# Low parts of the later experts' weights formed on GpSimd instead of VectorE, the opening tile's down weights split in two pieces, and the last tiles' table numbers read early on TensorE

## The reference, cut to what matters

```python
scores = sigmoid(xf @ gate_w + bias)
top_scores, top_idx = top_k(scores, 2)
w = zeros((T, 8)).at[arange(T)[:, None], top_idx].add(top_scores / (sum(top_scores) + 1e-06))
hact = gelu(einsum('th,ehi->tei', xf, up_w) + up_b)          # h = 256, i = 1024
eo = einsum('tei,eih->teh', hact, down_w) + down_b
combined = einsum('teh,te->th', eo * 0.1, w)
shared = (gelu(xf @ sw_up + sb_up) @ sw_down + sb_down) * 0.1
out = shared + combined
out = out / (max(abs(out), axis=-1) + 1e-06)
x = x + gb * out
```

## Time and profile before

| | us |
|---|---|
| median of 3 runs | 867.51 |
| lowest and highest of them | 866.81 and 871.16 |
| the profiled execution, device time | 869.19 |
| its span in the trace | 867.40 |

### The profile page before, as it was taken

The page is one execution under the profiler, slowest core; times in us unless marked ns, Lnnn a source line. Parts: engine busy times, 40 slices in busy tenths (PEclk is TensorE's granted clock), DMA queues, the critical chain, the costliest instruction groups (busy, mean ns, idle before and its releaser), DMA issues.

```text
span 867.4 us, 21209 instructions
## 1 busy us (share of the span) xinstructions
PE 830.5 (96%) x5973; PEld 777.6 (90%) x5974; DVE 612.7 (71%) x1570; ACT 454.6 (52%) x857; POOL 455.6 (53%) x519
## 2 busy tenths in 40 slices
PE   5999999999999999999989999989999999999993
PEld 5778887889899889888889999989999999999993
DVE  5688988567877687677776667657666667665664
ACT  3765565144444444443666556656555566655550
POOL 4354420124656655765503655554666665665675
PEclk9899999899999999999999999999999999999997
DMA  8220000090422432240671332352344443344543
GB/s 303 75 88 11 0 1 1 12 320 16 125 51 76 125 91 59 100 125 20 227 272 51 102 101 78 90 176 68 86 91 98 94 89 87 77 97 92 101 100 54
DMA packets 68392, 83.08 MB, mean 96 GB/s; under 512 B 22916, under 2 KB 56670, under 8 KB 68192
## 3 DMA queue, kind: packets, MB, share of 16 engines
q0 software_dynamic: 25696, 39.77, 19.7%
q1 hardware_dynamic: 41808, 41.64, 15.3%
q10 hardware_dynamic: 816, 0.79, 0.3%
HBM read 45.43 MB, written 41.29 MB: 100 GB/s over the span
## 4 chain that ended last, share of the span: by engine, by line
PE 59%; issue 6%; DMA 4%; DVE 4%; POOL 3%; ACT 2%; DVEq 1%; ACTq 1%; POOLq 0%; SPq 0%
PE psY L2000 15%; PE psUp L1975 15%; PE psU L1188 10%; PE psY L1200 9%; DMA gx<-shared_part,meta 2%; PE psZ L1128 1%; PE psO L1128 1%; DMA shared_part<-ys,widx 1%; PE psH L1941 1%; ACT gu L2044 1%; PE psZ L1116 1%; POOL out L2320 1%; PE psZ L1107 1%; PE psU L1151 1%; PE psZ L1138 1%
## 5 line engine op out<-in xcount | busy, mean ns | idle before, releaser
L1975 PE MATMUL psUp<-eT,wup 128*128 128x256 f32 x1632 | 204.4, 285 | 7.2 <-DVE eT L2101 4.7
L1975 PEld LDWEIGHTS psUp<-eT,wup 128*128 128x128 f32 x1632 | 200.3, 193 | 8.4 <-issue 8.1
L2000 PE MATMUL psY<-wdn,gTh 128*128 128x256 f32 x1088 | 200.5, 286 | 0.0
L2000 PEld LDWEIGHTS psY<-wdn,gTh 128*128 128x128 f32 x1088 | 169.4, 192 | 0.0
L2000 PE MATMUL psY<-wdn,gTl 128*128 128x256 f32 x544 | 154.3, 284 | 0.0
L2320 POOL DMA_INDIRECT out<-fin,oidx x68 | 109.2, 1606 | 25.4 <-issue 17.5
L2296 POOL DMA_INDIRECT gx<-shared_part,meta x68 | 67.3, 989 | 92.8 <-DMA shared_part<-ys,widx 63.7
L2044 ACT ACTIVATE gu<-psUp,ubias 128x256 f32<-128x256 f32 x272 | 113.4, 468 | 4.4 <-DVE gTl L2106 3.4
L2063 ACT ACTIVATE ys<-yc,meta 128x256 f32<-128x256 f32 x66 | 30.0, 503 | 152.1 <-DVE yc L2129 152.1
L2306 POOL DMA_INDIRECT shared_part<-ys,widx x66 | 68.9, 1044 | 71.8 <-issue 44.6
L2106 DVE TENSOR_TENSOR gTl<-gu,gTh 128x512 fp32r<-128x512 f32 x136 | 93.7, 689 | 18.2 <-ACT gTh L2049 15.6
(11 more groups left out here) (331 smaller groups left out, 1399.4 us busy)
## 6 DMA issues: line engine op xcount, KB each, us to landing
hin<-expert_in SPq DMA_DIRECT2D x36, 256.0 KB
X<-in_L_attn_x SPq DMA_DIRECT2D x8, 512.0 KB, 7.6
X<-bo_row POOLq DMA_DIRECT2D x8, 512.0 KB, 5.6
shared_part<-prow SPq DMA_DIRECT2D x8, 512.0 KB, 5.9
shared_part<-sh SPq DMA_DIRECT2D x8, 512.0 KB
out<-X SPq DMA_DIRECT2D x8, 512.0 KB, 4.7
raw_up<-in_L_ffn_up_w SPq DMA_DIRECT2D x3, 1024.0 KB, 5.2
raw_dn<-in_L_ffn_down_w SPq DMA_DIRECT2D x3, 1024.0 KB, 7.2
```

Source lines behind the costliest of these rows:

```text
L1975: mm = nc.tensor.matmul(psU[:, c, (m % 2) * TR:(m % 2 + 1) * TR], wup[s][:, a, k, m * P:(m + 1) * P], eT[:, u, b, k], start=(n == 0), stop ...
L2000: mm = nc.tensor.matmul(psE[:, u, h * C:(h + 1) * C], (gTh, gTl)[a][:, u, m, h * P:(h + 1) * P], wdn[s][:, b, m], start=(n == 0), stop=(n ...
```

## The change

`split_lo` can now run on GpSimd as well, and `ahead` for the low parts is taken out of VectorE's body and put into GpSimd's: the up weights ahead of the scatter, the down weights after the additions to `out`. GpSimd reads `ntab` in every tile for that, and VectorE no longer does. In the opening tile ScalarE does one chunk of gelu and high(1) first, then one piece of the down weights, a chunk, and the other piece; VectorE does low(1) right after the tables. SyncE waits for `w_ok` 2 before it loads either matrix of the second expert. On TensorE `early` reads `stab` of tiles 32 to 39 one by one in the two halves of tiles 0 to 3, and `ktab` of tiles 32 to 38 in tiles 30 and 31, two to a half; before, each was read two tiles ahead, between the matmuls of tiles 30 and later. `held` keeps the registers longer for that.

```diff
-    def split_lo(dve, n, s, which=(0, 1), halves=(0, 1)):
+    def split_lo(eng, n, s, which=(0, 1), halves=(0, 1)):
...
-                dve.wait_ge(w_hi, 4 * n + 2 * i + h + 1)
-                ins = nc.vector.tensor_tensor(lo[:, at], src[:, at], f32(hi[:, at]), ALU.subtract)
+                wait(eng, w_hi, 4 * n + 2 * i + h + 1)
+                unit = nc.gpsimd if eng.engine == nc.gpsimd.engine else nc.vector
+                ins = unit.tensor_tensor(lo[:, at], src[:, at], f32(hi[:, at]), ALU.subtract)
...
-        for old in [k for k in held if k[0] == eng.engine and k[2] < j - 2]:
+        for old in [k for k in held if k[0] == eng.engine and k[2] < j - 2 - ET + FULL]:
...
             with sp.If_ne(sp.to_reg(e), 0):
-                sp.wait_ge(w_ok, 1)
+                sp.wait_ge(w_ok, 2)
                 weights_up(sp, e)
-                sp.wait_ge(w_ok, 2)
                 weights_dn(sp, e)
...
+            def early(j, half):
+
+                if isinstance(j, int) and j < 4:
+                    n = 2 * j + half
+                    if FULL + n <= ET:
+                        known(pe, stab, FULL + n, 2)
+                elif isinstance(j, int) and FULL - 2 <= j < FULL:
+                    for n in (4 * (j - FULL + 2) + 2 * half, 4 * (j - FULL + 2) + 2 * half + 1):
+                        if FULL + n < ET:
+                            known(pe, ktab, FULL + n, E)
...
             def body(j, u, more, i):
-                soon = isinstance(j, int) and FULL - 2 <= j < ET - 2
-                if soon:
-                    known(pe, stab, j + 2, 2)
+                early(j, 0)
                 if more:
                     up(j + 1, 1 - u)
-                if soon:
-                    known(pe, ktab, j + 2, E)
+                early(j, 1)
                 down(j, u, more, i)
...
             high(0, 0)
-            split_hi(act, 0, 0, (1,))
-            chunks(0, 0, entry(act, etab, 0, E - 1), 2)
+            e_first = entry(act, etab, 0, E - 1)
+            chunk(0, 0, e_first, 0)
+            high(1, 1)
+            split_hi(act, 0, 0, (1,), (0,))
+            chunk(0, 0, e_first, 1)
+            split_hi(act, 0, 0, (1,), (1,))
+            chunk(0, 0, e_first, 2)
+            chunk(0, 0, e_first, 3)
...
             def body(j, u, more, i):
-                new = entry(dve, ntab, j, E - 1)
                 if later(j, 1):
                     start(j, u, i)
-                ahead(j, new, (0,))
...
                 targets(j, u, i)
-                ahead(j, new, (1,))
...
+            low(1, 1)
             low_g(0, 0, 0)
             split_lo(dve, 0, 0, (1,), (0,))
-            low(1, 1)
...
+            def ahead(j, new, which):
+
+                with pool.If_ne(pool.to_reg(new), 0):
+                    k = entry(pool, ktab, j, E)
+                    slot = known(pool, stab, j, 2)
+                    for s in range(2):
+                        with pool.If_eq(pool.to_reg(slot), 1 - s):
+                            split_lo(pool, k + 1, s, which)
+
             def body(j, u, more, i):
+                new = entry(pool, ntab, j, E - 1)
+
...
+                ahead(j, new, (0,))
                 wait(pool, ix_ok, 2 * j + 2)
...
+                ahead(j, new, (1,))
```

7 lines of the change are left out of this document (removed).

## The result

The changed kernel took 877.07 us (median of 4 runs, 876.23 to 878.03) against 867.16 us of the kernel before beside it (865.97 to 871.16). The ratio is 1.011, with a 95% interval from 1.0083 to 1.0138: it is slower by about 9.5 us. Its profiled execution took 876.63 us.

A forecast was written before the change was run, and what follows sets the result against it. TensorE, busy 96% of the span, was taken as the bound. Opening 2.85 and 0.8, tile 0 1.3, tile 10 3.0 and 0.5, loads 1.3, end -2.2 sum to +7.5 us: median 875.0, range 871 to 880.

The forecast's parts named there:

- tile 10's expert: Third expert's pairs make GpSimd 10.2 us late; TensorE waits at tiles 14 and 15: +3.0 us net, contention 0.5.
- SyncE's wait: Opening: the second expert's raw up weights go out only at about 446.7, so up(2) starts 2.6 us later.
- The pieces' cost on GpSimd: Each 128x1024 subtraction on GpSimd takes 2.55 us, a pair 5.1, four pairs 20.4 us.
- the contention behind the opening: GpSimd's subtractions delay VectorE instructions with two SBUF inputs: 0.5 us added in tile 10.
- (d): Exclusive lock by the letter: tile 10's pairs hold `gTl` up to 5.1 us each; another +4 to +6, 880 us; chance 0.10.
- TensorE's loads: A third table load per half in tiles 30 and 31 costs 0.5 us twice, tiles 0 to 3 0.3: together +1.3.
- The end: Tile 33 has no loads left, giving TensorE up to 4.2 us; the last gather limits the gain to -2.2 us.
- The slow restarts: After about 3 us of idleness TensorE's restart loses 1.5 us, after 1.2 to 1.35 none; two taken for tile 10.
- (a): GpSimd's lateness is absorbed and TensorE never waits for it in tile 10: -3.5 us, 864.0; chance 0.14.
- (c): Tile 10's wait moves without growing and tile 0's pair costs 0: +2.7 us, 870.2; chance 0.16.
- (b): The opening costs nothing either, weights landing before ScalarE gets there: -9.5 us, 858.0; chance 0.07.
- (e): GpSimd sets the pace, its cycle 12.15 us against 12.0 in each of 30 tiles: about +5 more, 880; chance 0.06.

The follow-up runs named there:

- e1: Changed kernel with the later experts' low parts back on VectorE, the rest as changed; ratio 1.0016 to the kernel before, +1.4 us.
- e10: Changed kernel with the low-part code of tiles 30 to 38, never executed there, given back from GpSimd to VectorE; ratio 1.008 to the kernel before.
- e5: Kernel before with only TensorE's early table loads added; ratio 1.0005 to the kernel before, no change.
- e2: Changed kernel with GpSimd forming low parts only in the loop, VectorE those in the unrolled tiles; ratio 1.0057 to the kernel before, +4.9 us.
- e11: Changed kernel with an expert's two down pieces apart, one behind each addition to `out`; ratio 1.007 to the kernel before.
- e4: Changed kernel with GpSimd filling zeros instead of subtracting, so it writes without reading; ratio 1.0042 to the kernel before, +3.6 us.
- e8: Changed kernel with each GpSimd piece cut into quarters, eight instructions for a matrix instead of two; ratio 1.0133 to the kernel before.
- e12: Kernel before with the reordered opening, `stab` read early and `ktab` one entry per half of tiles 30 to 33; 865.38 us against 869.90, ratio 0.9955.
- e3: Changed kernel with SyncE's two separate waits restored, the rest as changed; ratio 1.0066 to the kernel before.

## Why the prediction was right, and where not

The measured 877.07 us lie 2.1 above the predicted 875.0, on the side and within the range that were given; the working behind it held in part, and that the number came out so near is in part luck. By the traces, from up(0):

| step | forecast | trace | what the runs showed |
|---|---|---|---|
| opening, to up(3) | +2.85 and 0.8 | +3.60 | 2.1 to 3.9 in the seven traces with one wait; e1, no pair on GpSimd: 2.3 |
| tile 0's down pair | +1.3, at up(5) | +3.0, at up(4) | another mechanism; 1.5 in e10, with the same code |
| tile 10's expert | +3.0 and 0.5, at tiles 14 and 15 | +4.1, at tiles 13 and 14 | another mechanism |
| loads on TensorE | +1.3 | +1.1 | e5: 1.06 |
| end up to the last addition | -2.2 | -2.0 | e5: -1.3 |
| behind the last addition | nothing | +2.1 | GpSimd's code, e10 |
| sum | +7.5 | +11.9 | medians: +9.5 |

**SyncE's wait** was right, with its rows. In the changed kernel's trace:

```profile
442.04 0.38 SPq L1008 DMA_DIRECT2D raw_up<-in_L_ffn_up_w  x1
442.51 0.46 SPq L1011 DMA_DIRECT2D raw_dn<-in_L_ffn_down_w  x1
```
```profile
447.96 2.00 ACT L1021 CAST wup<-raw_up 128x1024 fp32r<-128x1024 f32 x2 [4.56 <-DMA raw_up<-in_L_ffn_up_w]
```

The issue is 10.37 us after up(0), forecast 10.6 (446.7 - 436.10); ScalarE begins 16.29 after up(0), forecast 15.8 to 16.4, and up(2) is 3.37 us late (forecast 2.6, and 0.8 for contention) after 4.69 us of idleness (forecast 4.0), with the slow restart. Two `gTl` were held there for 1.4 us. Most of the spread between traces is the time to landing: ScalarE began 5.0 us (e10) to 7.2 us (e2) after the issue. Where it began 5.0 to 5.2 us after, TensorE was 2.7 us late at up(3) with subtractions on GpSimd (e10, e11) and 2.1 and 2.3 without (e4, e1): the contention in the opening is worth about 0.5 us, not far from the 0.8 that were forecast.

**The pieces' cost on GpSimd** was right: 5.17 to 5.35 us a pair, half of it a piece, forecast 2.55. VectorE slows them little; where a `gTl` passed in the opening of e8, the quarter beside it took 1.18 us instead of 0.74.

**The step that failed is the contention behind the opening.** The prediction saw rows 8, took 0.5 us for tile 10 and nothing for tile 0's down pair, and let the pairs cost through the late gather. In the traces it is the other way round: `bs` is held for 4.4, 5.4 and 5.5 us beside these three pairs, and the idleness is one tile earlier than forecast. Two things were not seen. The prediction looked for `gTl` under a piece, but it is `bs` that stands there: GpSimd's pair comes right behind its additions to `out`, and in the same moment the gather issued before them lands and VectorE begins `bs`. And the hold was thought to be one piece at most (2.6 us); behind GpSimd's additions it lasts for the pair. The place where the late gather would tell was worked out rightly, as e4 shows by idleness at up(5), up(14) and up(15), but not its size in tile 10: there e4 is 0.8 us later behind the expert's tiles than ahead of them, where 3.0 were forecast, with fills that are 1 us shorter a pair and with one slow restart, not two. In the changed kernel it is covered by the larger stall. The rival (d), given 0.10, had the mechanism, though it put it on `gTl`.

The Trainium skill, SBUF — State Buffer, Who interferes with whom, says that a VectorE instruction with two inputs in SBUF and a GpSimd instruction that reads SBUF shut each other out, and that one that only writes does not. The traces agree on both (`bs` 0.69 us beside e4's fills, 5.10 to 6.17 beside the changed kernel's subtractions). That is said of the length of one instruction; behind GpSimd's additions the hold went on over two (changed kernel) and over nearly eight (e8), in the opening it did not.

**TensorE's loads**: the size was right (1.1 us, forecast 1.3), and three in a half do show, 0.63 and 0.43 us of idleness, where the kernel before took 0.15 and 0.21 us more than for the tiles ahead of them.

The Trainium skill, Advanced Engine Details and Errata, Engine Queue Depths, gives TensorE a queue of 64. Read as the prediction reads it, as work ahead that would hide the loads, it doesn't agree with these rows.

**The end**: TensorE won 4.4 us (forecast 4.2) and 2.0 arrived, the gather being last, as forecast: the last `bs` waited 2.27 us for it. What was missed is the 2.1 us behind it. No row before showed what longer code in the last tiles costs an engine that ends the span.

**The slow restarts**: the prediction put them behind "about 3 us" of idleness. The runs don't bear that out: there was none behind 2.94 us (the changed kernel, up(4)) and 2.97 us (e5, up(12)), and one behind 2.52 us (e12, up(12)). That two came behind tile 10, as was taken, doesn't bear the rule out.

**Why the number was near nevertheless.** The sum of the terms was 4.4 us too small. In the medians 2.4 of these are missing, 9.5 against 11.9 us: the profiled runs are single executions, and e10's trace, 1.3 us apart at up(10) with the same code, shows what that may hide. And the mechanism that was priced, with the hold taken out of it, is worth less than the forecast: e4 as a whole took 3.6 us more than the kernel before, with the 2 us at the end in it. The hold, which the forecast nearly left out, made up the rest.

The rivals: (a) needed no stall behind tile 12, and those at up(13) and up(14) are new; (c) needed these to cost no more than the 4.7 us that went, and tile 0's pair nothing, but they cost 4.1 us more, and tile 0's pair 3.0; (b) needed up(2) on time. (e) did not happen: where it has nothing to wait for, GpSimd's queue has 0.17 to 0.31 us between its instructions, as before.

## What to carry to other kernels

Before moving an operation from VectorE to GpSimd, list what VectorE does at that moment: in this kernel an addition with two SBUF inputs was held until GpSimd's pair of subtractions was through, so that 9.4 us taken off VectorE cost it 16.7. Cutting the GpSimd work smaller didn't help in the pairs right behind GpSimd's DMA issues, though it did in the opening. Look at what VectorE has due under each piece. Of a change in several parts, measure each alone: here the parts without GpSimd and without SyncE's merged wait, with the loads spread, made a kernel that measured 0.45% faster than the one before, though its trace doesn't show where.

## What had not been expected of the hardware

- A row of GpSimd reads right behind its DMA issues held VectorE almost as one: two `sm` 5.83 us beside eight subtractions in 6.35 us (e8); a DMA issue between two let it in (e11). In the opening it did not: there three `gTl` passed between the eight (e8), and in the changed kernel a `gTl` that became ready at 451.45, near the border of the first two pieces, passed in 0.70 us.
- Records of one engine can overlap: fills of 128x512 on GpSimd are shown with 0.53 us in the opening and 1.11 us right behind its DMA issues (e4), but in both places they start 0.47 us apart, and eight take 3.8 and 4.4 us. So the sum of single records is not the engine's time.
- Equal idleness was not followed by the same restart: 48 matmuls took 5.99 us after 2.22 us of idleness (e3, up(2)) and 7.48 after 2.23 (e4, up(15)).
- Code on GpSimd that is never executed, in the last tiles, lengthened the end by 2 us: the last branch took 2.5 to 2.8 us to its next instruction instead of 0.1 to 0.5, with an 8 KB packet of an instruction queue in between.
